# AdaLN block on one core: means subtracted on GpSimd, all engines' orders laid out anew

## What is computed

```python
h = _layernorm(x, axis=-1) * (1 + ca) + sa
x = x + ga * attn(h)
h = _layernorm(x, axis=-1) * (1 + cb) + sb
x = x + gb * ffn(h)
# attn, 16 heads of 8 features, reshaped to (b, h, dh, t) = (32, 16, 8, 256):
attn = jnp.einsum('bhdt,bhds->bhts', k, v) * temperature
attn = jax.nn.softmax(attn, axis=-1)
out = jnp.einsum('bhdt,bhts->bhds', q, attn)
# ffn: fp4_linear quantises both operands in blocks of 16 to an FP4 grid
h = silu(fp4_linear(x, w_gate)) * fp4_linear(x, w_up)
return fp4_linear(h, w_down)
```

## Time and profile before

| | us |
| --- | --- |
| median of 3 runs (lowest, highest) | 612.01 (610.42, 612.53) |
| span of the profiled execution | 611.3 |
| busy PE, DVE, ACT, POOL | 558.3, 568.7, 555.9, 507.3 |
| exponentials, ACT L825 ACTIVATE | 483.5 in 1024, mean 552 ns |
| maxima, DVE L1005 | 312.1 in 256, mean 1219 ns |
| scores, PE L1502 | 234.9 in 1024, mean 333 ns |
| mixes, PE L1548 | 132.6 in 2048 |

### The profile page before, as it was taken

How to read it: one execution, slowest core, us unless ns; L and a number is a source line. 1 busy time by engine, 2 the same in 40 slices (tenths; PEclk the granted TensorE clock), 3 DMA queues, 4 the chain that set the end, 5 groups by cost and what they waited for, 6 DMA issues and landing times.

```text
span 611.3 us, 15522 instructions
## 1 busy us (share of the span) xinstructions
PE 558.3 (91%) x4336; PEld 385.6 (63%) x4336; DVE 568.7 (93%) x1124; ACT 555.9 (91%) x2281; POOL 507.3 (83%) x710
## 2 busy tenths in 40 slices
PE   4588999999999999999999999999999999998874
PEld 2465556666666666666666666666666666666653
DVE  5568799999999999999999999999999999999986
ACT  2499899999999999999999999999999999999621
POOL 5544478999999999999999999999999999988741
PEclk9669899999999999999999999999999999999878
DMA  5655556546655556555655556655655556652000
GB/s 156 179 142 143 129 152 163 145 133 170 170 140 147 149 155 173 159 157 137 172 144 143 149 155 171 171 145 139 170 144 141 152 153 174 164 143 58 10 10 26
DMA packets 87888, 86.12 MB, mean 141 GB/s; under 512 B 8566, under 2 KB 83548, under 8 KB 87804
## 3 DMA queue, kind: packets, MB, share of 16 engines
q1 hardware_dynamic: 85372, 83.10, 50.4%
q10 hardware_dynamic: 2432, 2.03, 1.2%
HBM read 47.29 MB, written 37.81 MB: 139 GB/s over the span
## 4 chain that ended last, share of the span: by engine, by line
ACT 52%; PE 18%; issue 13%; DVE 12%; POOL 3%; ACTq 1%; DVEq 0%; POOLq 0%
ACT probs L825 47%; DVE neg_max L1005 6%; PE score_ps L1502 6%; PE bank L1581 5%; PE bank L1570 3%; ACT hT L835 2%; DVE silu_g L1123 2%; ACT hid_T L859 2%; PE bank L1548 2%; PE bank L1606 1%; ACT q_T L841 1%; DVE h_mag L975 1%; POOL hid_q L367 1%; PE bank L1520 1%; DVE h_mag L979 1%
## 5 line engine op out<-in xcount | busy, mean ns | idle before, releaser
L825 ACT ACTIVATE probs<-score_ps,neg_max 128x256 f32<-128x256 f32 x1024 | 483.5, 552 | 5.4 <-DVE neg_max L1005 4.3
L1005 DVE TENSOR_REDUCE neg_max<-score_ps 128x4 f32<-128x1024 f32 x256 | 312.1, 1219 | 19.5 <-PE score_ps L1502 16.8
L825 ACT ACTIVATION_READ_ACCUMULATOR probs<-score_ps,neg_max 128x1 f32 x1024 | 292.4, 286 | 0.0
L1502 PE MATMUL score_ps<-v_stack,k_stack 128*128 128x256 f32 x1024 | 234.9, 333 | 24.2 <-ACT probs L825 21.7
L1502 PEld LDWEIGHTS score_ps<-v_stack,k_stack 128*128 128x128 f32 x1024 | 156.0, 194 | 108.2 <-ACT probs L825 85.1
L1548 PE MATMUL bank<-probs,q_z 128*32 128x256 f32 x2048 | 132.6, 389 | 0.0
L1548 PEld LDWEIGHTS bank<-probs,q_z 128*32 128x32 f32 x2048 | 57.6, 111 | 42.4 <-issue 3.2
L1606 PEld LDWEIGHTS bank<-wd_T,hid_T 118*128 118x128 f32 x384 | 52.7, 201 | 7.6 <-ACT hid_T L859 1.3
L1606 PE MATMUL bank<-wd_T,hid_T 118*128 118x128 f32 x384 | 56.0, 286 | 0.5 <-ACT hid_T L859 0.5
L1570 PE MATMUL bank<-wgu_T,h_T 128*128 128x352 f32 x128 | 52.0, 488 | 1.7 <-ACT h_T L848 0.5
L367 POOL TENSOR_TENSOR hid_q<-hid_r,hid_sc 128x704 f32<-128x704 bf16 x31 | 43.0, 1387 | 7.6 <-DVE hid_r L362 7.5
(11 more groups left out here) (119 smaller groups left out, 880.9 us busy)
## 6 DMA issues: line engine op xcount, KB each, us to landing
split_dram<-kv_hi SPq DMA_DIRECT2D x124, 128.0 KB, 2.6
split_dram<-kv_lo SPq DMA_DIRECT2D x124, 128.0 KB, 2.6
k_stack<-split_dram SPq DMA_DIRECT2D x124, 128.0 KB, 4.5
v_stack<-split_dram SPq DMA_DIRECT2D x31, 512.0 KB, 4.2
mod_bc<-mod_dram SPq DMA_DIRECT2D x32, 256.0 KB, 4.0
x_in<-in_L_attn_x_dram SPq DMA_DIRECT2D x32, 128.0 KB, 3.1
out_dram<-out_t SPq DMA_DIRECT2D x32, 128.0 KB, 3.6
split_dram<-kv_hi ACTq DMA_DIRECT2D x4, 128.0 KB, 2.4
```

The costliest lines, as they stand in the source:

```text
L825: nc.scalar.activation(probs[p][:, h, a, :], score_ps[:, j % 4, a, :], ACT.Exp, bias=neg_max[:, p, n:n + 1], accum_out=row_sum[:, p, h, a: ...
L1005: nc.vector.tensor_reduce(neg_max[:, p, 4 * u:4 * u + 4], score_ps[:, lo:lo + 2, :, :].rearrange("p b a n -> p (b a) n"), AX.X, ALU.max, n ...
L1502: done = nc.tensor.matmul(score_ps[:, j % 4, a, :], k_stack[p][:, h, 128 * a:128 * a + 128], v_stack[p][:, h // R, :], start=True, stop=True)
```

## The change

`nm1`, `nm2` and `minus_mean` go; the three places that normalise read the mean from the statistics and subtract it. `wait_bank` gets one list per case in place of all earlier readers. The lists of all five queues are in a new order, with lags counted anew, and the lists of the last batches too; PSUM tiles stay in their banks. `gates` on PE gets a semaphore of its own.

```diff
...
+        def mean_of(stats, c, a):
+
+            return stats[:, c % 2, 1 + 3 * a:2 + 3 * a]
...
-                wait_batches(pool, nm1_made, b + 1)
                 wait_batches(pool, xT_made, b)
                 for a in range(2):
-                    nc.gpsimd.tensor_scalar(xn[:, a, :], x_in[:, b % NX, a, :],
-                                            nm1[:, a:a + 1], rstd1[:, a:a + 1],
-                                            ALU.add, ALU.mult).then_inc(xn_made, 1)
+                    nc.gpsimd.tensor_scalar(xn[:, a, :], x_in[:, b % NX, a, :], mean_of(stats1, c, a),
+                                            rstd1[:, a:a + 1], ALU.subtract, ALU.mult).then_inc(xn_made, 1)
...
                 variance(var1, stats1, c % 2).then_inc(var1_made, 1)
-                wait_batches(dve, xn_made, b, 2)
-                minus_mean(nm1, stats1, c % 2).then_inc(nm1_made, 1)
...
-            def wait_bank(b, latest, *older):
-
-                for s, n in (*latest, *older):
+            def wait_bank(b, before, others={}):
+
+                for s, n in others.get(b, before):
                     wait_batches(pe, s, n)
```

PE's step after (the step before it is printed above):

```diff
+                at(k, 9, up_proj, 1)
+                at(k, 11, down_proj, 1)
+                at(k, 6, scores, 0)
+                if k == 8:
+                    ff_transpose(1)
+                at(k, 9, up_proj, 0)
+                at(k, 6, scores, 1)
+                at(k, 9, gate_proj, 0)
+                at(k, 6, scores, 2)
+                at(k, 9, gate_proj, 1)
+                at(k, 6, scores, 3)
+                at(k, 6, scores, 4)
+                at(k, 7, mix, 0)
+                at(k, 6, scores, 5)
+                at(k, 7, mix, 1)
+                if k == 1:
                     condition()
+                at(k, 7, mix, 2)
+                at(k, 7, mix, 3)
+                at(k, 6, scores, 6)
+                at(k, 7, mix, 4)
+                at(k, 6, scores, 7)
+                at(k, 7, mix, 5)
+                at(k, 4, x_transpose)
+                at(k, 7, mix, 6)
+                at(k, 7, mix, 7)
+                at(k, 6, scores, 8)
+                at(k, 6, scores, 9)
+                if k == 8:
+                    ff_transpose(0)
+                at(k, 4, kv_proj)
+                at(k, 6, scores, 10)
+                at(k, 10, hid_transpose, 1)
+                at(k, 10, hid_transpose, 0)
+                if k == 4:
+                    gates()
+                at(k, 6, scores, 11)
+                if k == 9:
                     ff_transpose(2)
+                at(k, 6, scores, 12)
+                at(k, 6, scores, 13)
+                at(k, 8, h2_transpose)
+                at(k, 10, down_proj, 0)
+                at(k, 6, scores, 14)
+                at(k, 4, q_proj)
+                at(k, 6, scores, 15)
```

ACT's step after:

```diff
+                at(k, 6, exps, 14)
+                at(k, 4, load_k_stack)
+                at(k, 6, exps, 15)
+                at(k, 8, tanh, 0)
+                at(k, 5, exps, 0)
+                if k == 1:
+                    biases()
+                at(k, 5, exps, 1)
+                if k == 7:
+                    ff_out(1)
+                at(k, 8, tanh, 1)
+                at(k, 5, exps, 2)
+                at(k, 5, exps, 3)
+                at(k, 5, exps, 4)
+                at(k, 5, exps, 5)
+                at(k, 3, h_out)
+                at(k, 5, exps, 6)
+                if k == 4:
+                    load_first_ka()
+                at(k, 5, exps, 7)
+                if k == 4:
                     load_first_va()
+                at(k, 5, exps, 8)
+                if k == 7:
+                    ff_out(0)
+                at(k, 5, exps, 9)
                 if k == 8:
                     ff_out(2)
+                at(k, 9, hidT_out, 1)
+                at(k, 9, hidT_out, 0)
+                at(k, 3, store_v_hi)
+                at(k, 3, store_v_lo)
+                at(k, 5, exps, 10)
+                at(k, 5, exps, 11)
+                at(k, 7, h2T_out)
+                at(k, 5, exps, 12)
+                at(k, 5, exps, 13)
+                at(k, 3, q_out)
             for k in range(TAIL):
                 step(k)
```

DVE's step after, without the tasks on the weights:

```diff
+                at(k, 7, maxes, 6)
+                at(k, 5, k_lo)
+                at(k, 10, hid_exponent)
+                at(k, 5, v_lo)
+                at(k, 7, maxes, 7)
...
+                at(k, 3, stats1_rows)
+                at(k, 10, hid_magic)
...
+                at(k, 11, gate2)
...
+                at(k, 6, maxes, 0)
...
+                at(k, 8, h2_max)
+                at(k, 7, row_sums_inv)
...
+                at(k, 3, variance1)
+                at(k, 9, silu, 0)
...
+                at(k, 6, maxes, 1)
...
+                at(k, 8, h2_recip)
+                at(k, 9, times_up, 0)
+                at(k, 6, maxes, 2)
+                at(k, 9, silu, 1)
...
+                at(k, 9, times_up, 1)
+                at(k, 8, h2_exponent)
+                at(k, 6, maxes, 3)
+                at(k, 8, h2_magic)
+                at(k, 7, gate1)
+                at(k, 6, maxes, 4)
+                at(k, 9, hid_max)
+                at(k, 4, k_hi)
+                at(k, 6, maxes, 5)
+                at(k, 9, hid_recip)
+                at(k, 7, stats2_rows)
+                at(k, 4, v_hi)
+                at(k, 7, variance2)
...
```

On SP the loads of x (`load_x`) move to the head of the step with a shorter lag, and the stores and loads of keys and values keep their order among themselves but for single places. On POOL the tasks on the weights are spread over steps 4 to 8: `ff_scale(1)` stands in step 4, while DVE has `ff_max(1)` in its step 6. The last lists of PE do heads 4 to 9 of batches 30 and 31 and the mixes between them in this order:

```diff
+            last(mix, 29, 0)
+            last(scores, 30, 4)
+            last(scores, 30, 5)
+            last(mix, 29, 1)
+            last(mix, 29, 2)
+            last(mix, 29, 3)
+            last(scores, 30, 6)
+            last(scores, 30, 7)
             last(hid_transpose, 26, 1)
+            last(scores, 30, 8)
+            last(mix, 29, 4)
+            last(scores, 30, 9)
...
             last(scores, 31, 4)
+            last(scores, 31, 5)
             last(mix, 30, 0)
-            last(scores, 31, 5)
             last(mix, 30, 1)
             last(mix, 30, 2)
-            last(mix, 30, 3)
             last(scores, 31, 6)
             last(scores, 31, 7)
+            last(mix, 30, 3)
             last(mix, 30, 4)
+            last(scores, 31, 8)
             last(mix, 30, 5)
+            last(scores, 31, 9)
             last(mix, 30, 6)
             last(mix, 30, 7)
...
             last(scores, 31, 12)
+            last(down_proj, 27, 0)
             last(scores, 31, 13)
...
             last(h2_transpose, 29)
             last(down_proj, 27, 1)
+            last(scores, 31, 14)
```

More of the change, by code:

```diff
@@ L745, in _ @@
             last(residual1, 30)
-            last(h2_sub, 29)
             last(h2_rescale, 29)
@@ L903, in _ @@
+                at(k, 3, q_out)
             for k in range(TAIL):
                 step(k)
+            last(exps, 30, 14)
+            last(exps, 30, 15)
+            last(tanh, 28, 0)
+            last(exps, 31, 0)
+            last(exps, 31, 1)
+            last(tanh, 28, 1)
+            last(exps, 31, 2)
+            last(exps, 31, 3)
+            last(exps, 31, 4)
+            last(exps, 31, 5)
+            last(exps, 31, 6)
+            last(exps, 31, 7)
+            last(exps, 31, 8)
+            last(hidT_out, 27, 0)
@@ L905, in _ @@
+            last(exps, 31, 9)
             last(hidT_out, 27, 1)
+            last(exps, 31, 10)
             last(h2T_out, 29)
+            last(exps, 31, 11)
+            last(tanh, 29, 0)
             last(exps, 31, 12)
-            last(tanh, 29, 0)
             last(exps, 31, 13)
@@ L915, in _ @@
             last(h2T_out, 30)
+            last(tanh, 30, 1)
             last(tanh, 30, 0)
-            last(tanh, 30, 1)
             last(hidT_out, 29, 0)
@@ L1330, in _ @@
+            last(maxes, 30, 0)
+            last(gate2, 25)
+            last(h2_max, 28)
+            last(row_sums_inv, 29)
+            last(silu, 27, 0)
+            last(maxes, 30, 1)
+            last(h2_recip, 28)
+            last(silu, 27, 1)
+            last(maxes, 30, 2)
+            last(times_up, 27, 1)
+            last(h2_exponent, 28)
+            last(maxes, 30, 3)
+            last(times_up, 27, 0)
+            last(h2_magic, 28)
+            last(maxes, 30, 4)
             last(hid_max, 27)
@@ L1665, in _ @@
                 step(k)
-            last(hid_transpose, 26, 1)
+            last(up_proj, 27, 1)
+            last(scores, 30, 0)
+            last(down_proj, 25, 1)
+            last(scores, 30, 1)
+            last(gate_proj, 27, 0)
+            last(scores, 30, 2)
+            last(scores, 30, 3)
+            last(up_proj, 27, 0)
+            last(gate_proj, 27, 1)
+            last(mix, 29, 0)
[3 more added lines that the diff above has]
+            last(mix, 29, 2)
@@ L1667, in _ @@
+            last(mix, 29, 3)
+            last(scores, 30, 6)
+            last(scores, 30, 7)
+            last(hid_transpose, 26, 1)
+            last(scores, 30, 8)
+            last(mix, 29, 4)
+            last(scores, 30, 9)
+            last(mix, 29, 5)
+            last(scores, 30, 10)
+            last(mix, 29, 6)
+            last(mix, 29, 7)
```

(6 more changed lines are left out.)

539 lines of the change are left out of this document (216 added, 323 removed).

## The result

The changed kernel takes 710.12 us (median of 4 runs, 709.43 to 712.66) against 612.27 before (median of 4 too): a ratio of 1.162, 95% interval 1.158 to 1.166. The direction was forecast, the size was not: 643.5 was forecast and 652 was the upper end. The profiled span is 708.8 us, against 611.3.

A forecast was written before the change was run, and what follows sets the result against it. ACT was seen as having no room, with a loop of scores, maxima and exponentials to watch. Span 611.3 + 32.5 (batches) - 1.0 (end) = 642.8, plus 0.7 from span to median: 643.5 us; range 622 to 652.

The forecast's parts named there:

- Part 1: Negated means dropped, GpSimd subtracting: no cost taken, -0.1 to +0.1 us a batch; at most the 0.28 bubble won.
- the heads' loop: Scores on PE, maxima on DVE, exponentials on ACT, four PSUM slots: expected to set the batch at 18.30 us.
- Part 3: PE's steady order of heads and mixes: head 0 to head 8 takes 9.50 us, not 7.93; +32.5 us over 29 batches.
- the rest of the batch: ACT's work from head 8 to the next head 0: 8.80 us, with DVE's 16.6 us of work fitting in 18.3.
- The bound of +0.2: Upper allowance for DVE's maxima after head 8 in a nearly full queue, giving 18.5 us a batch.
- rival C: TensorE's clock falls in mid-run: 7.1 us per such batch, 21 us in three of 29, 665 us; chance 0.07.
- Rival A: PE's switches between scores and mixes are hidden, ACT sets a 16.90 us batch: 602.9 us; chance 0.12.
- rival B: Comes out even: switches partly hidden, DVE's saved time used, batch 17.2 us, 611 to 614 us; chance 0.05.
- A steady batch: Head 0 to the next head 0: 9.50 + 8.80 = 18.30 us, 1.12 more than before.
- start: Time to the first exponential, at 24.59 us before: change taken as 0, bounds -2 and +2 us.
- end: ACT's waits within batch 31, 1.93 us: 1.0 us of them taken as saved, bounds 0 and 3.
- Part 2: Fewer semaphores in waits before PE's bank groups: 0, at most what PE's issue gaps hide.

The follow-up runs named there:

- experiments 3: Kernel before, VectorE's reductions kept but the mean stored unnegated and subtracted by GpSimd: 647.34 us.
- experiment 4: Kernel before, VectorE's reductions kept but unused, GpSimd adding the mean read from the statistics: 613.13 us.
- experiment 1: Changed kernel with VectorE's negated means back and GpSimd adding them, all new orders kept: 665.67 us, ratio 1.084.
- experiment 8: Kernel before with mixes 5 to 7 ahead of heads 8 and 9 on TensorE instead of behind them: 655.99 us, ratio 1.072.
- experiment 7: Kernel before with the same five mixes ahead of heads 8 and 9 in four blocks instead of two: 646.08 us, ratio 1.056.
- experiments 2: Kernel before with only the first edit: no negated means, GpSimd subtracts the mean from the statistics: 647.18 us, ratio 1.054.
- experiment 9: Changed kernel with GpSimd scaling q earlier and VectorE's row-sum reciprocals ahead of h2's maxima: 665.32 us, ratio 1.087.
- experiment 11: Kernel before, x's variance, negated mean and h2's rounding constant behind heads 6 and 7's maxima, mix 4 behind head 9, GpSimd additions reordered: 634.73 us.

## Why the prediction was wrong

**Part 1** is the step that failed: "same instruction, same shape, no cost taken (between -0.1 and +0.1 us a batch, POOL has 7 us in 100 free)". The instruction is not the same, its operation differs, and it takes 0.80 us instead of 0.45 (experiments 3 and 4): 1.4 us a batch, above the free 1.21. (Between the rows of before and after it is 1.26, because 27 of the 62 additions on h_c took 0.62 and not 0.45 before.) No row of the trace before showed a GpSimd subtraction with a scalar operand, so the bound had to come from somewhere wider. I had also looked at GpSimd's share alone. The loop mix 7, gated product, residual, GpSimd's queue, scaled q, mix 0 could be followed in the order of the change; with 12.01 us of queue it is 19.29, and with 1.4 less 17.9, under the heads' loop of 18.33.

**Part 3**, the order of heads and mixes, held in mechanism and nearly in size: 9.42 us in experiment 1, where nothing else disturbs it, and 9.43 in the kernel after once the two new terms are taken out, against 9.50. What failed in it is the rest of the batch, 8.80, in experiment 1 (9.37): "DVE has 98.5% of 17.18 less 0.29, 16.6 us of work, in 18.3" counted VectorE's work but not that it stands waiting in the first half and then has a solid queue, nor that its 16-bit instruction can be held up beside GpSimd. The bound of +0.2 I had set for that queue was too small by 0.4. In the kernel after, without the reductions, the rest was 8.90.

**The clock** was rival C, given 0.07 and 665 us. It came, in three batches of four and at 1.59 us each, not 7.1: the low level lasts 3.4 us, not the whole of PE's part. Priced this way, in three quarters of 29 batches, C would have been 643.5 + 22 x 1.59 = 678. I had argued from PE's busy share over a batch; the fall follows waits in one place (0.76 and 0.95 us, within 2.2 us). Not every such wait is followed by one: in the batch at 265.83 the same two waits are 0.76 and 0.94 and the clock stays up. The 1.27 us of experiment 8 are followed by a fall in some batches and not in others too. What decides between them stays open. Rival A (changes hidden) is refuted by PE's rows above and by experiment 7, rival B with it. The weight loads ahead of matmuls in flight that the Trainium skill, "TensorE: Matmul & The Clock Gate", Architectural detail, allows do not show behind the mixes here: a head behind a single mix takes 0.43 us, not 0.24.

**The sum.** A steady batch was to be 18.30. It is 20.48 in the mean (three of 20.88, one of 19.30): 0.97 for q, 3/4 x 1.59 = 1.19 for the clock, +0.02 for all else, 2.18 in all. By the forecast's own terms, the 97.4 us of span divide so. The **start** was taken as 0 and costs 2.2 (first exponential at 26.8, 24.6 before). From there to the first exponentials of batch 30 it is 89.9 more (606.8 against 516.9), where 32.5 were forecast. The **end**, from those exponentials on, was taken as -1.0 and costs 5.3 (75.2 us remain, 69.8 before). Why the start is late stays open: in experiments 2 and 3 the subtraction alone puts the first exponential at 26.3 and 26.5, but experiment 1, with the addition back, has it at 26.7 as well. **Part 2**, the shorter waits for banks, leaves nothing in a steady batch (the 0.02), as forecast; it was not run alone.

The range missed because part 1 had no price and the rivals were priced one at a time: no case held a slower GpSimd and falls of the clock together. Taking away the subtraction (experiment 1) or the wait that it causes (experiment 9) gives back 44 to 45 of the 67 us between forecast and result, the clock's falls included. The other 22 stay with the new orders. In experiment 1 they are 2.1 at the start, 14.4 up to batch 30, above all VectorE's queue (0.57 a batch), and 5.3 from batch 30 on. The lower end of the range was also summed short: 623 with the start and the end at their bounds is 619, not 622; nothing hung on it.

## What to carry to other kernels

Where one engine's order is changed, follow every loop that passes through it, the one over the slowest side engine too, and add up its queue between the two ends: the longest loop sets the period, and one that is less than 1 us short of it can be the longest after the next edit. Never take an ALU operation as free because the instruction and its shape stay; time it, or bound it widely: here the factor was 1.8. And before an idle gap is filled, look at what runs on the other engines in it.

## What the runs showed of the hardware

- GpSimd's two-operation instruction on 128 x 128 f32 takes 0.80 us with subtract first and 0.45 with add first, whichever tile holds the scalar (experiments 2 to 4). The first of each pair on h_c took 0.62 with add (kernel before, experiment 4) and 0.97 with subtract (experiments 2 and 3), again 0.35 more.
- VectorE's 16-bit tensor_scalar instructions, 0.29 and 0.33 us, took up to 1.45 (experiment 11) and 0.86 us (experiment 1) when GpSimd was at work beside them, and so a wait of GpSimd can be worth keeping. The trace shows the delay as busy time, not as a wait.
- The low clock after a wait of TensorE lasted 3.4 us in mid-run and cost 1.59 us in the kernel after; removing one wait of 0.95 us removed all of it from the steady batches (experiments 1 and 9). Like waits were not always followed by it (0.76 and 0.94 us in the kernel after, 1.27 in experiment 8).
